# First pass of a four-layer graph kernel: statistics of two chunks of x earlier, a group's tail one chunk later, the weights' split in three pieces

## The chip, the core and the metric

One core of a Trainium2 chip. The metric is device time in microseconds (us) of one launch. TensorE is called PE below, VectorE DVE, ScalarE ACT, GpSimd POOL, and SyncE, which issues nearly all transfers, SP.

## What is computed

x has 4096 rows of 256, adj is a dense 4096 x 4096 matrix. Four graph layers follow each other, each with a layer norm before it and a residual behind it:

```python
h = relu(layernorm(x)); x = x + L0(h, adj, W)
    # L0: A2 = adj + I; d = diag(A2)**-0.5
    #     relu((d[:,None]*A2*d[None,:]) @ (A2 @ h @ W.T))
h = relu(layernorm(x)); x = x + L1(h, adj, weight, bias)   # softmax attention, weighted by adj
h = relu(layernorm(x)); x = x + L2(h, adj, W, b)           # relu(D^-1/2 adj D^-1/2 h @ W + b)
h = relu(layernorm(x)); x = x + L3(h, adj, W1, W2)         # two relu(concat(h, adj @ h) @ W)
```

All inputs and the output are f32.

## The kernel before

**Six passes over adj.** Each pass multiplies adj with a 4096 x 256 matrix: pass 0 is `A2 @ h` of the first layer, pass 1 its second product, pass 2 the attention, pass 3 the third layer, passes 4 and 5 the last one. An f32 matrix goes to PE as two f16 halves, hi (ACT, with a scale) and lo (DVE: the scaled value less hi), and a product is three matmuls: hi with hi, hi with lo, lo with hi.

**The first pass** (`first_pass`, L1206) is the only one that the change touches. adj is cut into 8 groups of 512 rows (`g`) and 8 chunks of 512 columns (`c`), 1 MB per chunk. The chunk (g, c) is loaded by SP into one of four ring slots (`load_at`, `load`), its hi half is made by ACT (L1487, in `split`), its lo half by DVE (L1939, in DVE's `split`); PE then runs 24 matmuls over 512 columns (`turned_block`, L1171 to 1173), or 48 over 256 and 128 columns if c equals g (`beside_corner`, L1186 to 1188), since the blocks on the diagonal, which get the identity added, are done apart (`corner_blocks`, L1203, after c = 7). From group 2 on DVE also makes two sums of quarters of each chunk (L1946, L1948) for later passes. Groups 0 and 1 (`PAIRED` = 2) run interleaved: chunk number n = 2c + g, so that n = 0 is (0, 0), n = 1 is (1, 0), n = 2 is (0, 1). From group 2 on n = 8g + c. PE takes the chunks in the order of n.

**The rows of x.** In group 0 chunk c of adj needs the normalised rows of chunk c of x (also 512 rows). They are made on the way, in a chain over three engines: DVE takes the statistics (`norm_stats`, the stage "stats" with p = PRE: bn_stats L2260 four times, bn_aggr L2265, L2267, L2268), POOL makes the power -1/2 and the shift (`rstd_of`, L1016, L1019), ACT writes relu of the normalised row in f16 and the normalised row in f32 (`first_rows`, L1631 and L1634, four rows of 128 each), and DVE makes the low half (L2081 row by row for chunks 0 to 2, L2093 for four at a time from chunk 3 on). PE waits for them row by row in chunks 0 to 2.

**Chunk 0** of adj comes in two halves: ACT makes two hi halves, DVE two lo halves (`split_first`, L2045), and PE begins its second half (k = 2) when the second is there.

**The tail of a group** is the product of its result with the layer's weights and its scaling. Its first half, "z", turns the sums in PSUM into hi and lo (ACT L1603, DVE L2052); PE then runs a small product (L1295 to 1297) after c = 2 of the next group; the second half, "t", turns its result into the moving matrix of pass 1 (ACT L1620, DVE L2069). `FIRST_PLACES` says behind which chunk of the next group ACT and DVE do each; the table stands once in ACT's program and once in DVE's. The groups 0 and 1 have their tails in group 2, by `TWO_PLACES`. The groups 4 to 7 are a loop, `first_group` twice per turn. The tail of group 7 lies in pass 1's first group, by the same table.

**The weights.** The first layer's are split early; the others (`wofs[1]` to `wofs[5]`, 3072 columns in one tensor) behind c = 5 of group 3, by one ACT instruction (L1460) and one DVE instruction (L2531). `w_ready` counts DVE's splits; POOL, PE and DVE wait for 2 before what follows.

**What sets the order.** Each engine has its own program, written out by hand, and works through it in order; semaphores tie them together. An engine that waits holds up everything behind it on that engine. So the order of DVE's program decides when each split and each row is ready.

Of the kernel before, what the change touches and what calls it, by code (L numbers as in the profile page):

```python
# [63 lines left out]
PAIRED = 2  # L64
# [6 lines left out]
PRE = -1  # L71
# [11 lines left out]
def build(nc, x, adj_t, w0, wg, bias_g, w2, bias_2, w3a, w3b, sent, sums, ready, x_mid, directs, out):  # L83
# [4 lines left out]
    with ctx:  # L88
# [125 lines left out]
        w_loaded = sem("w_loaded")  # L214
# [123 lines left out]

        PLAIN = [0, 1]

        def chunk_no(p, g, c):
# [661 lines left out]
        def _(pool):  # L1003
# [58 lines left out]
            add_identity(PAIRED + 1, 1)  # L1062
            pool.wait_ge(w_ready, 2)
            nc.gpsimd.memset(mov[1][:, :, F:LO], 1.0).then_inc(ones_ready, 1)
# [11 lines left out]
        def _(pe):  # L1076
# [350 lines left out]
            for p in range(6):  # L1427
                if p == 1:

                    pe.wait_ge(w_ready, 2)  # L1430
                    pe.wait_ge(ones_ready, 2)
# [22 lines left out]
        def _(act):  # L1454
# [344 lines left out]

            FIRST_PLACES = {0: "z", 3: "t"}  # L1800
            TWO_PLACES = {0: ("z", 0), 3: ("t", 0), 4: ("z", 1), 7: ("t", 1)}

            def first_group(g, side):

                for c in range(NC):
# [6 lines left out]
                    if c == 6:  # L1812
                        hi_of_corner(g, side)
                    if isinstance(g, int) and g == PAIRED + 1 and c == 5:
                        hi_of_weights(slice(wofs[1], wofs[5]), w_loaded, 16 * 4)

# [109 lines left out]
        def _(dve):  # L1926
# [498 lines left out]

            FIRST_PLACES = {0: "z", 3: "t"}
            TWO_PLACES = {0: ("z", 0), 3: ("t", 0), 4: ("z", 1), 7: ("t", 1)}

            def first_group(g, side):

                for c in range(NC):
# [6 lines left out]
                    if c == 6:  # L2438
                        lo_of_corner(g, side)
                    if isinstance(g, int) and g == PAIRED + 1 and c == 5:  # L2440
                        lo_of_weights(slice(wofs[1], wofs[5]), 2)

# [96 lines left out]
            lo_of_first_row(0, 0)  # L2539
            lo_of_first_row(0, 1)  # L2540
            split_first(1, split_ready, split_hi)
            lo_of_first_row(0, 2)
            lo_of_first_row(0, 3)
            stage("stats", PRE, 1)
            for q in range(NG):
                if q > 0:
                    split(0, 0, q)
                if q == 1:
                    lo_of_first_rows(1)
                    stage("stats", PRE, 2)  # L2550
                elif q == 2:
                    stage("stats", PRE, 3)
                    lo_of_first_rows(2)
                elif q > 2 and q + 2 < NG:
                    stage("stats", PRE, q + 2)
                elif q == NG - 1:
                    lo_of_corner(0, 0)
# [18 lines left out]
            dve.wait_ge(b_loaded, 32)  # L2576
            dve.wait_ge(w_ready, 2)
            for p in range(6):
# [56 lines left out]
```

## Time and profile before

| | us |
|---|---|
| median of 3 runs | 2312.75 |
| lowest and highest | 2312.53, 2313.29 |
| the profiled execution | 2313.05 |
| its span | 2311.3 |
| PE busy | 2289.8 (99%) |
| DVE busy | 1693.5 (73%) |
| ACT busy | 1127.9 (49%) |
| POOL busy | 145.9 (6%) |

The span runs from the first to the last instruction in the trace of one execution; its own time is that of the whole launch. In a row of the trace's order of time the first number is the start in us from the span's start, the second how long the row lasted; then follow engine, line, operation, what it writes and reads, the shape, and, in brackets, if the engine was idle before it, the idle time with what released it. A row of a stretch gives its start and end, its length, then the busy time and instructions of PE, PE's weight loads, DVE, ACT and POOL, the granted clock as a share of full speed, the busy share of the DMA engines and GB/s. A row of transfers gives what they move, their number, their size and the us from issue to landing.

### The profile page before, as it was taken

The page shows a single profiled execution, that of the slowest core. Times are in us where ns is not written, and L with a number is a line of the kernel's source. Part 1 is how long each engine was busy: PE and PEld are TensorE (multiplying, and loading weights), DVE is VectorE, ACT ScalarE, POOL GpSimd, SP SyncE. Part 2 cuts the span into 40 slices and gives each one's busy share as a digit, 9 for nine tenths or more (in the row PEclk, how much of TensorE's full clock was granted, in tenths as well). Part 3 has the DMA queues.
Part 4 walks back from the last instruction along what each step waited for, and adds up shares of the span by engine and source line. Part 5 has one row for each costly group of instructions (what it writes and reads, how often), then busy time and mean ns, then how long its engine had stood idle before and what let it go on. Part 6 is the DMA issues. An engine that isn't in the chain of part 4 may idle for free.

```text
span 2311.3 us, 61483 instructions
## 1 busy us (share of the span) xinstructions
PE 2289.8 (99%) x24200; PEld 1896.5 (82%) x24200; DVE 1693.5 (73%) x2709; ACT 1127.9 (49%) x1806; POOL 145.9 (6%) x139
## 2 busy tenths in 40 slices
PE   7999999999999999999999999999999999999999
PEld 4555557888888677778888899999988888899999
DVE  7678677676677788778888876776766667667666
ACT  7444434445544555555555555455454444433332
POOL 3300110111111000000000000000000000000000
PEclk9999999999999999999999999999999999999999
DMA  9989998889887898989999998998998998999998
GB/s 336 334 276 330 350 337 305 284 261 281 264 268 229 261 287 288 288 270 312 333 310 330 338 351 310 332 330 310 331 349 307 330 343 301 340 344 383 374 377 301
DMA packets 294894, 727.17 MB, mean 315 GB/s; under 512 B 77024, under 2 KB 114656, under 8 KB 262112
## 3 DMA queue, kind: packets, MB, share of 16 engines
q1 hardware_dynamic: 294608, 724.95, 90.6%
q8 instruction: 97, 1.59, 0.3%
q14 instruction: 45, 0.37, 0.0%
q10 hardware_dynamic: 144, 0.26, 0.0%
HBM read 574.64 MB, written 138.41 MB: 309 GB/s over the span
## 4 chain that ended last, share of the span: by engine, by line
PE 90%; DVE 5%; issue 2%; ACT 1%; DMA 1%; POOL 0%; SPq 0%; DVEq 0%; POOLq 0%; ACTq 0%
PE acc L1084 9%; PE acc L1086 8%; PE acc L1085 8%; PE acc L1110 8%; PE acc L1106 8%; PE acc L1109 8%; PE acc L1096 4%; PE acc L1099 4%; PE acc L1098 4%; PE acc L1171 4%; PE acc L1172 4%; PE acc L1173 4%; PE psS L1389 2%; PE psS L1391 2%; PE psS L1390 2%
## 5 line engine op out<-in xcount | busy, mean ns | idle before, releaser
L1084 PE MATMUL acc<-right,ahi 128*128 128x258 f16 x1024 | 279.7, 273 | 3.2 <-DVE alo L2502 2.8
L1086 PE MATMUL acc<-right,alo 128*128 128x258 f16 x1024 | 279.6, 273 | 0.0
L1085 PE MATMUL acc<-right,ahi 128*128 128x256 f16 x1024 | 279.1, 273 | 0.0
L1106 PE MATMUL acc<-left,ahi 128*128 128x128 f16 x1536 | 270.5, 219 | 0.4 <-DVE alo L2020 0.4
L1109 PE MATMUL acc<-left,ahi 128*128 128x128 f16 x1536 | 270.4, 219 | 0.0
L1110 PE MATMUL acc<-left,alo 128*128 128x128 f16 x1536 | 270.4, 219 | 0.0
L1867 ACT ACTIVATE ahi<-en 128x512 f16<-128x512 f32 x256 | 160.2, 626 | 76.2 <-DVE en L2487 74.0
L2502 DVE SCALAR_TENSOR_TENSOR alo<-en,ahi 128x512 f16<-128x512 f32 x256 | 176.0, 687 | 4.1 <-ACT ahi L1867 4.1
L1106 PE MATMUL acc<-left,adj 128*128 128x128 f16 x1024 | 178.2, 219 | 0.0
L1106 PE MATMUL acc<-left,en 128*128 128x128 f16 x1024 | 178.2, 219 | 0.0
L1109 PE MATMUL acc<-left,adj 128*128 128x128 f16 x1024 | 178.2, 219 | 0.0
L1109 PE MATMUL acc<-left,en 128*128 128x128 f16 x1024 | 178.2, 219 | 0.0
L1110 PE MATMUL acc<-left,adj 128*128 128x128 f16 x1024 | 178.2, 219 | 0.0
L1110 PE MATMUL acc<-left,en 128*128 128x128 f16 x1024 | 178.2, 219 | 0.0
L1106 PEld LDWEIGHTS acc<-left,ahi 128*128 128x128 f16 x1536 | 150.3, 98 | 0.7 <-DVE alo L2020 0.6
L1109 PEld LDWEIGHTS acc<-left,ahi 128*128 128x128 f16 x1536 | 150.3, 98 | 0.0
L1110 PEld LDWEIGHTS acc<-left,alo 128*128 128x128 f16 x1536 | 150.3, 98 | 0.0
L1548 ACT ACTIVATE ahi<-en 128x512 f16<-128x512 f32 x191 | 118.6, 621 | 54.6 <-DVE en L2015 54.5
L1084 PE MATMUL acc<-left,ahi 128*128 128x258 f16 x512 | 139.8, 273 | 0.0
L1086 PE MATMUL acc<-left,alo 128*128 128x258 f16 x512 | 139.8, 273 | 0.0
L1084 PE MATMUL acc<-left,en 128*128 128x258 f16 x512 | 139.8, 273 | 0.0
L1086 PE MATMUL acc<-left,en 128*128 128x258 f16 x512 | 139.8, 273 | 0.0
(313 smaller groups left out, 7036.9 us busy)
## 6 DMA issues: line engine op xcount, KB each, us to landing
adj<-in_adj_t SPq DMA_DIRECT2D x194, 512.0 KB, 5.8
adj<-ready SPq DMA_DIRECT2D x96, 1024.0 KB, 7.8
en<-ready SPq DMA_DIRECT2D x96, 1024.0 KB, 8.2
en<-in_adj_t SPq DMA_DIRECT2D x32, 1024.0 KB, 8.9
adj<-in_adj_t SPq DMA_DIRECT2D x31, 1024.0 KB, 7.5
en<-ready SPq DMA_DIRECT2D x56, 512.0 KB, 5.4
en<-sent SPq DMA_DIRECT2D x46, 512.0 KB, 7.2
sent<-en SPq DMA_DIRECT2D x90, 256.0 KB, 4.1
```

The source lines that it names most:

```text
L1084: nc.tensor.matmul(acc[:, b, 0:n], hi, m[:, jb, 0:n], start=first, stop=False)
L1085: nc.tensor.matmul(acc[:, b, 0:F], hi, m[:, jb, LO:LO + F], start=False, stop=False)
L1086: return nc.tensor.matmul(acc[:, b, 0:n], lo, m[:, jb, 0:n], start=False, stop=last)
L1096: nc.tensor.matmul(to, bhi[:, cols], hi[:, rows], start=first and i % 2 == 0 and k == 0, stop=False, skip_group_check=True)
L1098: nc.tensor.matmul(to, bhi[:, cols], lo[:, rows], start=False, stop=False, skip_group_check=True)
L1099: last = nc.tensor.matmul(to, blo[:, cols], hi[:, rows], start=False, stop=False, skip_group_check=True)
L1106: nc.tensor.matmul(to, hi[:, rows], bhi[:, cols], start=first and i % 2 == 0 and b == 0 and k == 0, stop=False, skip_group_check=True)
L1109: nc.tensor.matmul(to, hi[:, rows], blo[:, cols], start=False, stop=False, skip_group_check=True)
L1110: last = nc.tensor.matmul(to, lo[:, rows], bhi[:, cols], start=False, stop=False, skip_group_check=True)
L1548: nc.scalar.activation(ahi[:, c % 2, 2 * QUAD:3 * QUAD], s1_of(p, g, c), ACT.Copy, scale=ADJ_SCALE)\
L1867: nc.scalar.activation(ahi[:, (j // GB) % 2, j % GB * GR:(j % GB + 1) * GR], nums[:, n % NUMS, :], ACT.Copy, scale=P_SCALE).then_inc(num_h ...
L2502: nc.vector.scalar_tensor_tensor(alo[:, (j // GB) % 2, cols], nums[:, n % NUMS, :], P_SCALE, ahi[:, (j // GB) % 2, cols], ALU.mult, ALU.su ...
```

## The change

Four edits, all in the first pass:

1. DVE takes the statistics of x chunk 1 before the second half of adj chunk 0 and the low halves of rows 2 and 3, where it took them behind these.
2. DVE takes the statistics of x chunk 2 before the low halves of chunk 1, where it took them behind these.
3. `FIRST_PLACES` puts "t" behind c = 4 and not c = 3, on ACT and DVE, for groups 3 to 7 and for pass 1's first group.
4. The split of the later weights, one piece behind c = 5 of group 3, becomes three of 1024 columns each behind c = 1, 3 and 7 (`WEIGHTS_AT`), on ACT and DVE; the waits for `w_ready` 2 become waits for 4.

```diff
+        WEIGHTS_AT = {1: (wofs[1], wofs[3]), 3: (wofs[3], wofs[4]), 7: (wofs[4], wofs[5])}
...
-            pool.wait_ge(w_ready, 2)
+            pool.wait_ge(w_ready, 4)
...
-                    pe.wait_ge(w_ready, 2)
+                    pe.wait_ge(w_ready, 4)
...
-            FIRST_PLACES = {0: "z", 3: "t"}
+            FIRST_PLACES = {0: "z", 4: "t"}
...
-                    if isinstance(g, int) and g == PAIRED + 1 and c == 5:
-                        hi_of_weights(slice(wofs[1], wofs[5]), w_loaded, 16 * 4)
+                    if isinstance(g, int) and g == PAIRED + 1 and c in WEIGHTS_AT:
+                        hi_of_weights(slice(*WEIGHTS_AT[c]), w_loaded, 16 * 4)
...
-                    if isinstance(g, int) and g == PAIRED + 1 and c == 5:
-                        lo_of_weights(slice(wofs[1], wofs[5]), 2)
+                    if isinstance(g, int) and g == PAIRED + 1 and c in WEIGHTS_AT:
+                        lo_of_weights(slice(*WEIGHTS_AT[c]), 2 + list(WEIGHTS_AT).index(c))
...
             lo_of_first_row(0, 0)
             lo_of_first_row(0, 1)
+            stage("stats", PRE, 1)
             split_first(1, split_ready, split_hi)
             lo_of_first_row(0, 2)
             lo_of_first_row(0, 3)
-            stage("stats", PRE, 1)
             for q in range(NG):
                 if q > 0:
                     split(0, 0, q)
                 if q == 1:
+                    stage("stats", PRE, 2)
                     lo_of_first_rows(1)
-                    stage("stats", PRE, 2)
                 elif q == 2:
                     stage("stats", PRE, 3)
                     lo_of_first_rows(2)
```

The edit of `FIRST_PLACES` stands twice, once for ACT and once for DVE; so does the wait of DVE for `w_ready`. All lines behind the first edit move down by one.

**DVE at the start of the program.** `alo` of 128x1024 is a half of adj chunk 0, `alo` and `right` of 128x2048 are whole chunks (L1939), `right` of 128x256 are low halves of rows of x. Before, from the first half on:

```order
L2045 SCALAR_TENSOR_TENSOR alo<-adj,ahi 128x1024
L2081 SCALAR_TENSOR_TENSOR right<-o,right 128x256 x2
L2045 SCALAR_TENSOR_TENSOR alo<-adj,ahi 128x1024
L2081 SCALAR_TENSOR_TENSOR right<-o,right 128x256 x2
L2260 BN_STATS stats<-left 128x6 x4
L2265 BN_AGGR mv<-stats 128x2 x4
L2267 TENSOR_SCALAR nmean<-mv 128x4
L2268 TENSOR_SCALAR vare<-mv 128x4
L1939 SCALAR_TENSOR_TENSOR alo<-adj,ahi 128x2048
L1939 SCALAR_TENSOR_TENSOR right<-en,right 128x2048
L2081 SCALAR_TENSOR_TENSOR right<-en,right 128x256 x4
L2260 BN_STATS stats<-left 128x6 x4
```

Now:

```order
L2046 SCALAR_TENSOR_TENSOR alo<-adj,ahi 128x1024
L2082 SCALAR_TENSOR_TENSOR right<-o,right 128x256 x2
L2261 BN_STATS stats<-left 128x6 x4
L2266 BN_AGGR mv<-stats 128x2 x4
L2268 TENSOR_SCALAR nmean<-mv 128x4
L2269 TENSOR_SCALAR vare<-mv 128x4
L2046 SCALAR_TENSOR_TENSOR alo<-adj,ahi 128x1024
L2082 SCALAR_TENSOR_TENSOR right<-o,right 128x256 x2
L1940 SCALAR_TENSOR_TENSOR alo<-adj,ahi 128x2048
L1940 SCALAR_TENSOR_TENSOR right<-en,right 128x2048
L2261 BN_STATS stats<-left 128x6 x4
```

The four statistics instructions moved ahead of the second half of chunk 0 with its two rows; the next block of statistics moved ahead of the four low halves of chunk 1.

**DVE in group 3, behind c = 1.** `wsp` are the weights, `left<-psW` and `left<-psT` the tail's second half; each chunk is a split and two sums. Before, from c = 2 to the split of c = 4:

```order
L1939 SCALAR_TENSOR_TENSOR right<-en,right 128x2048
L1946 TENSOR_TENSOR right<-en 128x512
L1948 TENSOR_TENSOR right<-right,en 128x512
L1939 SCALAR_TENSOR_TENSOR right<-en,right 128x2048
L1946 TENSOR_TENSOR right<-en 128x512
L1948 TENSOR_TENSOR right<-right,en 128x512
L2069 SCALAR_TENSOR_TENSOR left<-psW,d_w,left 128x256 x2
L2069 SCALAR_TENSOR_TENSOR left<-psT,d_w,left 128x256 x2
L1939 SCALAR_TENSOR_TENSOR alo<-adj,ahi 128x2048
```

Now:

```order
L2532 SCALAR_TENSOR_TENSOR wsp<-left,wsp 128x1024
L1940 SCALAR_TENSOR_TENSOR right<-en,right 128x2048
L1947 TENSOR_TENSOR right<-en 128x512
L1949 TENSOR_TENSOR right<-right,en 128x512
L1940 SCALAR_TENSOR_TENSOR right<-en,right 128x2048
L1947 TENSOR_TENSOR right<-en 128x512
L1949 TENSOR_TENSOR right<-right,en 128x512
L2532 SCALAR_TENSOR_TENSOR wsp<-left,wsp 128x1024
L1940 SCALAR_TENSOR_TENSOR alo<-adj,ahi 128x2048
L1947 TENSOR_TENSOR right<-adj 128x512
L1949 TENSOR_TENSOR right<-right,adj 128x512
L2070 SCALAR_TENSOR_TENSOR left<-psW,d_w,left 128x256 x2
```

Two pieces of the weights stand ahead of the chunks c = 2 and c = 4, and the tail's second half moved behind c = 4. On ACT the same two moves are made.

## Rows read from the trace of the kernel before

**Rows 1.** Stretch from 371 us: PE, PEld, DVE, ACT, POOL busy (instructions), clock, DMA, GB/s

```profile
371.00:2311.30 1940.30, 1931.90 (x22072) 1704.24 (x22069) 1423.45 (x2392) 949.10 (x1621) 81.14 (x80) 1.00 0.91 312
```

**Rows 2.** The page: span, and granted TensorE clock in 40 slices

```profile
span 2311.3 us, 61483 instructions
...
PEclk9999999999999999999999999999999999999999
```

**Rows 3.** PE in order of time: first matmul of chunks 1 to 6

```profile
17.92 0.39 PE L1171 MATMUL acc<-ahi,right 128*128 128x512 f16 x1 [1.93 <-DVE alo L1939]
...
23.11 0.38 PE L1171 MATMUL acc<-right 128*128 128x512 f16 x1
...
29.02 0.28 PE L1186 MATMUL acc<-right 128*128 128x256 f16 x1 [0.57 <-DVE right L1939]
...
33.76 0.38 PE L1171 MATMUL acc<-ahi,right 128*128 128x512 f16 x1 [0.60 <-DVE right L2081]
...
39.49 0.39 PE L1171 MATMUL acc<-ahi,right 128*128 128x512 f16 x1 [0.39 <-DVE alo L1939]
...
46.41 0.39 PE L1171 MATMUL acc<-right 128*128 128x512 f16 x1 [1.57 <-DVE right L1939]
```

**Rows 4.** PE, first matmul of chunks 26, 27, 28, and of group 4's chunks three to five

```profile
158.25 0.38 PE L1171 MATMUL acc<-right 128*128 128x512 f16 x1
...
166.05 0.27 PE L1186 MATMUL acc<-right 128*128 128x256 f16 x1
...
171.27 0.39 PE L1171 MATMUL acc<-ahi,right 128*128 128x512 f16 x1 [1.10 <-DVE alo L1939]
...
211.50 0.38 PE L1171 MATMUL acc<-right 128*128 128x512 f16 x1
...
216.84 0.28 PE L1186 MATMUL acc<-ahi,right 128*128 128x256 f16 x1
...
220.81 0.38 PE L1171 MATMUL acc<-ahi,right 128*128 128x512 f16 x1
```

**Rows 5.** DVE in order of time, 11 to 22 us

```profile
11.50 1.22 DVE L2045 SCALAR_TENSOR_TENSOR alo<-adj,ahi 128x1024 f16<-128x1024 f32 x1
...
13.46 1.40 DVE L2260 BATCH_NORM_STATS2 stats<-left 128x6 f32<-128x256 f32 x4
...
15.57 2.29 DVE L1939 SCALAR_TENSOR_TENSOR alo<-adj,ahi 128x2048 f16<-128x2048 f32 x1
...
21.28 0.42 DVE L2081 SCALAR_TENSOR_TENSOR right<-en,right 128x256 f16<-128x256 f32 x1 [1.21 <-ACT en L1634]
```

**Rows 6.** ACT in order of time, 20 to 25 us

```profile
20.15 0.60 ACT L1631 ACTIVATE right<-left,shift,rstd 128x256 f16<-128x256 f32 x1 [3.46 <-POOL shift L1019]
...
24.10 1.89 ACT L1487 ACTIVATE right<-en 128x2048 f16<-128x2048 f32 x1
```

**Rows 7.** POOL in order of time, 15 to 34 us

```profile
15.75 2.98 POOL L1016 TENSOR_TENSOR rstd<-vare,neghalf 128x4 f32<-128x4 f32 x1 [7.56 <-DVE vare L2268]
...
33.36 1.11 POOL L1016 TENSOR_TENSOR rstd<-vare,neghalf 128x4 f32<-128x4 f32 x1 [2.14 <-DVE vare L2268]
```

**Rows 8.** DMA issues from 2.0 to 2.6 us, and landings of line 567's seven loads

```profile
left<-in_x SPq DMA_DIRECT2D x1, 512.0 KB, 6.7
...
DMA to landing us min/median/max: 6.7/10.2/13.9
```

**Rows 9.** PE: the warming matmuls, and where chunk 0's second half begins

```profile
6.95 4.42 PE L1420 MATMUL acc<-ident 128*128 128x128 f16 x40 [6.95 <-DVE vare L2268]
...
13.85 0.27 PE L1186 MATMUL acc<-ahi,right 128*128 128x256 f16 x1
```

**Rows 10.** DVE in order of time: splits of chunks 26 and 28, and the weights

```profile
154.51 2.28 DVE L1939 SCALAR_TENSOR_TENSOR right<-en,right 128x2048 f16<-128x2048 f32 x1
...
168.92 2.29 DVE L1939 SCALAR_TENSOR_TENSOR alo<-adj,ahi 128x2048 f16<-128x2048 f32 x1 [0.92 <-ACT ahi L1487]
...
175.99 3.35 DVE L2531 SCALAR_TENSOR_TENSOR wsp<-left,wsp 128x3072 f16<-128x3072 f32 x1
```

More of the change, by code:

```diff
@@ L2424, in first_tail @@
                     lo_of_t(g)
-            FIRST_PLACES = {0: "z", 3: "t"}
+            FIRST_PLACES = {0: "z", 4: "t"}
             TWO_PLACES = {0: ("z", 0), 3: ("t", 0), 4: ("z", 1), 7: ("t", 1)}
@@ L2576, in _ @@
             dve.wait_ge(b_loaded, 32)
-            dve.wait_ge(w_ready, 2)
+            dve.wait_ge(w_ready, 4)
             for p in range(6):
```

## The prediction, made before the changed kernel ran

> **What bounds the kernel now.** I read the page first, then the PE rows of the first pass in order of time, then what DVE, POOL and ACT did in front of each hole. PE is the clock of this program: in the 1940 us after the first pass it is busy for 1931.90 of 1940.30 us [rows 1], at a granted clock of full speed in every slice [rows 2]. A microsecond counts only if PE itself loses it, and the change touches only the first pass, so the question is how much PE loses there.
>
> To see that, one takes start to start, not the bracketed idle time, because a matmul's row overlaps the next by 0.16 us. An ordinary chunk of the first pass (24 matmuls over 512 columns) takes 23.11 - 17.92 = 5.19 us [rows 3]. The chunk on the diagonal (48 narrower ones) takes 220.81 - 216.84 = 3.97 us [rows 4]. I number chunks in PE's order: 0 to 15 are the paired groups 0 and 1, 24 to 31 are group 3. Against that:
> - chunk 2, 23.11 to 29.02: 5.91, so 0.72 lost before chunk 3
> - chunk 3 (diagonal), to 33.76: 4.74, so 0.77 lost before chunk 4
> - chunk 4, to 39.49: 5.73, so 0.54 lost
> - chunk 5, to 46.41: 6.92, so 1.73 lost
> - chunk 27 (diagonal), 166.05 to 171.27: 5.22, so 1.25 lost
> - group 4, its fourth chunk, 211.50 to 216.84: 5.34, so 0.15 lost, and the same in groups 5, 6 and 7.
>
> The releasers named in the brackets are DVE's splits (right or alo, L1939) and once a row of x (L2081) [rows 3, 4]. So in the early holes DVE is late. Why it is late stands in three views. DVE is out of work for 1.21 us at 21.28, waiting for ACT's normalised rows of x chunk 1 [rows 5]; ACT had waited 3.46 us for POOL's shift [rows 6]; and POOL's power took 2.98 us beside a DVE split, where a later one took 1.11 [rows 7]. It is one chain: statistics, power, rows, low halves, next split.
>
> **The change, part by part.**
>
> *Statistics of chunk 1 ahead of the second half of adjacency chunk 0.* The block of statistics costs DVE 15.57 - 13.46 = 2.11 us, the half split 1.22 [rows 5]. The block now starts at 11.50, so its x must have landed: that load was issued at 2.15 and took 6.7 us [rows 8], there at 8.9. The half split then runs 13.61 to 14.83 and two rows of 0.42 follow; DVE's work up to 15.57 is the same, so chunk 1's split still starts at 15.57 and PE still starts chunk 1 at 17.92. The price is that PE, which went on with chunk 0's second half at 13.85 [rows 9], now waits until about 15.2. That half took 2.1 us (to 17.92 - 1.93 = 15.99 [rows 3]), so it ends near 17.3, before 17.92: the hole of 1.93 us is cut in two and the term is **0**. Nothing else is queued behind it on PE.
>
> POOL gets the variance at 13.6 and not 15.6. Bounds: 1.11 us for the power if DVE leaves it alone, 2.98 if not [rows 7]. In both cases shift is there by about 17.9 at the latest, since DVE's next long split ends at 17.86 [rows 5]. ACT is free at 20.15 - 3.46 = 16.7 and needs 24.10 - 20.15 = 3.95 us for the eight activations of a chunk [rows 6]: done between 20.6 and 21.9, against 24.1.
>
> *Statistics of chunk 2 ahead of the low halves of chunk 1.* DVE is done with chunk 2's split at 15.57 + 2 x 2.29 = 20.15 and goes straight on: statistics to 22.26 (its x, issued at 3.8, landed by 17.7 even with the longest landing of all, 13.9 us [rows 8]), four low halves of 0.42 to 23.9, all inputs there. The rest, with the same durations, ACT's 1.89 for a split [rows 6], and PE's need from 17.92 on:
> - chunk 3: split done 26.2, PE needs it at 28.3: the 0.72 goes
> - chunk 4: split 28.5, statistics of chunk 3 30.6, first row 31.1, needed at 32.3: the 0.77 goes
> - chunk 5: rows to 32.3, split 34.6, needed at 37.5: the 0.54 goes
> - chunk 6: ACT reaches its rows of x chunk 3 at 33.4 (rows of chunk 2 to 29.6, two splits), or 35.5 if POOL is held up twice; rows done 37.4 to 39.5, DVE's low half about 1.2, split 2.29: done 40.9 to 43.0, needed at 42.7. The 1.73 goes, or 0.3 of it stays.
>
> Later paired chunks have what they need earlier too, since SP reissues a ring slot as soon as DVE has split it. Sum: 0.72 + 0.77 + 0.54 + 1.73 = **3.76 us**. Late next is chunk 6, with 1.8 us to spare or none.
>
> The SBUF page of the Trainium skill (SBUF — State Buffer, "Who interferes with whom") says that a DVE instruction with two SBUF inputs and a GpSimd one that reads SBUF exclude each other for a whole instruction, and that issue order decides who blocks. Here the long power rows fit the case in which DVE was first [rows 7]. By the rule the other order is possible too, and by it DVE would be set back by a whole power before chunk 1: the sum would be 4.5 and not 5.6, the second rival below.
>
> *A tail's second half one place later.* In group 3 chunk 28's split stood behind the tail's low halves and started only at 168.92 [rows 10]; PE wanted it at 166.05 + 3.97 = 170.0 [rows 4]. Now it goes ahead of the tail. Its adjacency chunk is requested right after chunk 24's split, some 20 us before, so only DVE's queue decides. Two chunks cost DVE 175.99 - 168.92 = 7.07 us there, 3.54 each [rows 10]: chunk 26 from 155.7 (with the piece of the weights below), chunk 27 to 162.8, the second piece to 164.0, chunk 28's split done at 166.3. Chunk 29 stands behind the tail now: sums to 167.6, four low halves of about 0.5 to 169.6, split done 171.9, needed at 170.0 + 5.19 = 175.2. **1.25 us** go, and in groups 4 to 7 4 x 0.15 = **0.6 us**. The tail's own result is not needed before the next tail, 211.50 - 166.05 = 45 us on [rows 4], or the next pass. In the second pass's first group the tail also moves; PE has no hole there, so 0. The cover is the 5.19 us that each chunk gives DVE.
>
> *The weights in three pieces.* 3.35 us in one instruction of 3072 columns [rows 10] become three of about 1.12 to 1.22 (the 1024-column form [rows 5]); the work is the same. Behind chunk 25 the first piece puts chunk 26's split at 154.51 + 1.22 [rows 10], done 158.02, and PE takes it at 158.25 [rows 4]: covered by 0.2 us, the thinnest place of the change. If POOL's identity additions stretch it, 0.1 to 0.3 us are lost. The second piece is in the times above, the third stands at the group's end, where DVE leads by 4 us. POOL's and PE's waits for four instead of two increments end near 181 against an end of the pass at 371: 0. Alone this part is worth 0.
>
> **Sum.** 3.76 + 1.25 + 0.6 = 5.6 us off, of which I take all. The profiled execution took 2313.05 us (span 2311.3), the median of the runs is 2312.75, 0.3 less; 2312.75 - 5.6 = **2307.1 us**. A measurement of this kernel tells apart some 0.2%, 4.6 us, so "faster" begins below 2308.1, and there is 1 us of room.
>
> **Rivals.**
> - *The gain is partly given back later* (0.13). DMA is 0.91 busy in the later stretch and PE idles 8.4 us there [rows 1]. If some of those idle spots are set by transfers that do not move with PE, they grow. For it: the high share. Against it: transfers start when a buffer comes free, so they move along, and 8.4 us in 1940 is little. Half of it given back: 2309.9.
> - *POOL or the thin places take their share* (0.13). DVE is held by a power that starts first (1.1), or chunks 6 and 26 come late (0.3 each). Against: beside the power at 15.75 the DVE split at 15.57 took its usual 2.29 [rows 5, 7]. About 1.2 us less: 2308.3.
> - *The clock falls* (0.05). PE began at the lower level, 40 matmuls over 128 columns in 4.42 us, 0.11 us each, that is 1.2 GHz [rows 9]; 5.19/24 = 0.216 us for 512 columns is 2.4 GHz [rows 3]. The new hole comes at 13.85, shortly after the rise. If the clock falls back there for as long as it took to rise, at most 13.85 - 6.95 = 6.9 us, PE loses half of that, 3.45, less the 0.7 that it has in hand before chunk 1: 2307.1 + 2.8 = 2309.9. Against: a hole of 1.93 us at 16 was followed by full speed, and now it is split into 1.35 and 0.6. The page TensorE: Matmul & The Clock Gate of the Trainium skill ("What's actually happening") has the level depend on how busy PE has lately been; by that rule too the shorter holes are the milder case.
> - *Slower than before* (0.03). The same fall, but lasting: from the point where more than 2 x (5.6 + 0.7) = 12.6 us run at half rate the change loses. At 20 us PE loses 10, less the 0.7: 2307.1 + 9.3 = 2316.4. The rows speak against it, since after chunk 1 PE would be without holes, and it rose once from a start that was no busier.
> - *It does not do what it says*: the statistics come sooner, but rows of x do not, because POOL is held until the same split ends. Then only the later terms stay, 1.85 us: 2310.9 (0.04). Even the fully blocked case above gains 2.2 us on ACT, so I give it little.
>
> **The numbers.** The forecast (0.62) has 2306.4 to 2308.1 as its own range. Reaching to the first three rivals gives 2305.9 to 2310.0. Faster takes the forecast and a third of the second rival, 0.66; slower 0.03; the rest 0.31.
>
> **What would show it.** Right: PE rows at 17.9, 23.1, 28.3, 32.3, 37.5, 42.7 without brackets but for the first, a hole of about 1.3 us near 14, ACT's rows of chunk 1 starting by 17.9, chunk 28 starting 3.97 us behind chunk 27. Wrong: chunk 1 later than 18.2, a hole before chunk 6 or 26, matmul rows of 0.42 us after 13, or PE idle after the first pass above 9 us.

## The result, and the profile after

| | before | after |
|---|---|---|
| median, 13 runs each | 2312.75 us | 2307.0 us |
| lowest and highest | 2312.19, 2313.29 | 2306.12, 2308.56 |
| the profiled execution | 2313.05 | 2306.9 |
| its span | 2311.3 | 2305.0 |

The ratio is 0.9976, with a 95% interval of 0.9969 to 0.9983: 5.75 us off, where 5.6 were forecast. The gain is clear of 1, but the interval reaches over 0.998, the line below which the prediction counts a kernel as faster, so the measurement does not settle that.

The stretch from the start of the second pass to the end, in the columns of [rows 1]:

```profile
365.00:2305.00 1940.00, 1931.96 (x22075) 1704.44 (x22072) 1422.44 (x2392) 948.63 (x1622) 81.15 (x80) 1.00 0.90 312
```

PE is busy for 1931.96 of 1940.00 us, before for 1931.90 of 1940.30. Its idle time went from 8.40 to 8.04 us, and the DMA share from 0.91 to 0.90. Nothing was given back later, so nearly all of the gain lies in the first pass. A hole is a stretch in which PE is idle; its bracketed time stands in the row of the matmul behind it. PE in the first pass, in order of time, the first matmul of each stage (the first row shows the warming matmuls, the second is the second half of chunk 0, then come chunks 1 to 6):

```profile
7.02 4.42 PE L1421 MATMUL acc<-ident 128*128 128x128 f16 x40 [7.02 <-DVE vare L2269]
...
15.43 0.28 PE L1187 MATMUL acc<-ahi,right 128*128 128x256 f16 x1 [1.43 <-DVE right L2082]
...
17.96 0.39 PE L1172 MATMUL acc<-ahi,right 128*128 128x512 f16 x1 [0.38 <-DVE alo L1940]
...
23.15 0.38 PE L1172 MATMUL acc<-right 128*128 128x512 f16 x1
...
28.33 0.27 PE L1187 MATMUL acc<-right 128*128 128x256 f16 x1
...
32.29 0.38 PE L1172 MATMUL acc<-ahi,right 128*128 128x512 f16 x1
...
37.47 0.38 PE L1172 MATMUL acc<-ahi,right 128*128 128x512 f16 x1
...
42.65 0.38 PE L1172 MATMUL acc<-right 128*128 128x512 f16 x1
```

Against [rows 3] the four holes before chunks 3 to 6 are gone. From chunk 1 on the starts are 5.18 or 5.19 us apart, 3.96 for the diagonal chunk 3. Chunk 6 starts at 42.65 and not at 46.41, 3.76 us sooner. The hole of 1.93 us before chunk 1 has become one of 1.43 inside chunk 0 and one of 0.38 before chunk 1, and chunk 1 starts where it did.

Group 3 and group 4 (chunks 26, 27 and 28, then group 4's fourth chunk and the diagonal one behind it), against [rows 4]:

```profile
154.34 0.38 PE L1172 MATMUL acc<-right 128*128 128x512 f16 x1
...
162.14 0.27 PE L1187 MATMUL acc<-right 128*128 128x256 f16 x1
...
166.10 0.38 PE L1172 MATMUL acc<-ahi,right 128*128 128x512 f16 x1
...
206.32 0.38 PE L1172 MATMUL acc<-right 128*128 128x512 f16 x1
...
211.50 0.27 PE L1187 MATMUL acc<-ahi,right 128*128 128x256 f16 x1
```

Chunk 28 stands 3.96 us behind chunk 27, where it stood 5.22 behind. The step of 5.34 in group 4 is 5.18 now, and the like losses of groups 5 to 7, in front of 261.19, 305.53 and 349.88 before, are gone too. Counting the lead from stage to stage, in starts of PE: 3.76 us at chunk 6, 3.91 at chunk 27, 5.17 at chunk 28, 5.34 at group 4's diagonal chunk, 5.76 at the first matmul of the second pass (370.73 before, 364.97 now).

DVE at the same place, the first piece of the weights, the splits of chunks 26 and 28 and the tail, against [rows 10]:

```profile
150.53 1.22 DVE L2532 SCALAR_TENSOR_TENSOR wsp<-left,wsp 128x1024 f16<-128x1024 f32 x1
151.67 2.28 DVE L1940 SCALAR_TENSOR_TENSOR right<-en,right 128x2048 f16<-128x2048 f32 x1
...
159.86 2.28 DVE L1940 SCALAR_TENSOR_TENSOR alo<-adj,ahi 128x2048 f16<-128x2048 f32 x1
...
163.39 0.87 DVE L2070 SCALAR_TENSOR_TENSOR left<-psW,d_w,left 128x256 f16<-128x256 f32 x2
```

Chunk 28's split is done at 162.14, 4 us ahead of PE; it was begun at 168.92 before. Chunk 26's is done at 153.95, 0.4 ahead.

DVE and ACT show why the early holes went. DVE, against [rows 5]:

```profile
11.71 1.40 DVE L2261 BATCH_NORM_STATS2 stats<-left 128x6 f32<-128x256 f32 x4
...
13.82 1.22 DVE L2046 SCALAR_TENSOR_TENSOR alo<-adj,ahi 128x1024 f16<-128x1024 f32 x1
...
15.62 2.28 DVE L1940 SCALAR_TENSOR_TENSOR alo<-adj,ahi 128x2048 f16<-128x2048 f32 x1
...
22.14 1.42 DVE L2082 SCALAR_TENSOR_TENSOR right<-en,right 128x256 f16<-128x256 f32 x4
23.87 2.29 DVE L1940 SCALAR_TENSOR_TENSOR right<-en,right 128x2048 f16<-128x2048 f32 x1 [0.31 <-ACT right L1488]
26.08 2.28 DVE L1940 SCALAR_TENSOR_TENSOR alo<-adj,ahi 128x2048 f16<-128x2048 f32 x1
...
39.39 2.28 DVE L1940 SCALAR_TENSOR_TENSOR right<-en,right 128x2048 f16<-128x2048 f32 x1
```

ACT and POOL, against [rows 6, 7]:

```profile
18.00 0.60 ACT L1632 ACTIVATE right<-left,shift,rstd 128x256 f16<-128x256 f32 x1 [1.10 <-POOL shift L1020]
```

```profile
13.99 1.92 POOL L1017 TENSOR_TENSOR rstd<-vare,neghalf 128x4 f32<-128x4 f32 x1 [5.74 <-DVE vare L2269]
15.98 1.98 POOL L1020 TENSOR_TENSOR shift<-nmean,rstd 128x4 f32<-128x4 f32 x1
22.31 1.11 POOL L1017 TENSOR_TENSOR rstd<-vare,neghalf 128x4 f32<-128x4 f32 x1 [4.34 <-DVE vare L2269]
```

The statistics of chunk 1 now start at 11.71 in place of 13.46, and ACT's rows of chunk 1 at 18.00 in place of 20.15. DVE's four low halves, which waited 1.21 us for ACT, now wait for nothing: they stand behind the statistics of chunk 2 and start at 22.14, and by then the rows are there. Chunk 6's split is done at 41.67, and PE takes it at 42.65: 1 us to spare.

### The profile page after: what moved, and what is told of

The parts are those of the page before. It is cut to its first block, busy times and chain, and to the rows that moved or that the text cites. A ratio compares the mean times of both kernels' runs of the same rounds, so it can differ in the third digit from the quotient of the medians.

```text
span 2305.0 us, 61487 instructions
## 1 busy us (share of the span) xinstructions
PE 2288.1 (99%) x24200; PEld 1897.1 (82%) x24200; DVE 1689.4 (73%) x2711; ACT 1129.0 (49%) x1808; POOL 139.7 (6%) x139
## 4 chain that ended last, share of the span: by engine, by line
PE 94%; DVE 4%; issue 1%; ACT 0%; DMA 0%; SPq 0%; DVEq 0%; ACTq 0%
PE acc L1085 9%; PE acc L1087 9%; PE acc L1086 9%; PE acc L1107 8%; PE acc L1110 8%; PE acc L1111 8%; PE acc L1097 4%; PE acc L1100 4%; PE acc L1099 4%; PE acc L1172 4%; PE acc L1174 4%; PE acc L1173 4%; PE psS L1390 2%; PE psS L1392 2%; PE psS L1391 2%; DVE alo L2503 1%
```

## The experiments

They were timed in four sets, each beside the kernel before, whose median was 2313.03, 2313.04, 2312.93 and 2312.71 us (33, 27, 24 and 14 runs). The sets ran on chips 5, 1, 0 and 5. The interval of each ratio reaches 0.0009 or 0.001 to either side, about 2 us. A difference between two of these kernels that is smaller than that is not settled by the medians; where it is called shown below, it is by the rows of the traces.

### The parts alone

**The two moves of the statistics alone.** The tables are as before:

```diff
-            FIRST_PLACES = {0: "z", 4: "t"}
+            FIRST_PLACES = {0: "z", 3: "t"}
...
-                    if isinstance(g, int) and g == PAIRED + 1 and c in WEIGHTS_AT:
+                    if isinstance(g, int) and g == PAIRED + 1 and c == 5:
```

> Only the two blocks of statistics are moved. Theory (DVE is late in the first 50 us and the rows of x are why): the four holes of PE before chunks 3 to 6 go, 3.8 us, and those near 171 us and of 0.15 us in groups 4 to 7 stay: 2309.0 us, chunk 1 starting at 17.9 as before, a hole of about 1.4 us near 14. Rival (the gain sits in the later stage, the tail's place and the weights): at most 1 us, 2311.8 or more. Rival (clock): some executions are 1 to 3 us above the others.

Measured: 2309.06 us (11 runs, ratio 0.9984, 0.9975 to 0.9993), 3.97 less than before, as expected. The early holes are gone, and the hole before chunk 28 stands as it was:

```profile
167.31 0.39 PE L1171 MATMUL acc<-ahi,right 128*128 128x512 f16 x1 [1.09 <-DVE alo L1939]
```

**The tail one chunk later alone.** `FIRST_PLACES` as in the change, all else as before.

> Only the tail's second half is moved from behind the fourth to behind the fifth chunk; the weights stay one piece. Theory: 1.25 us before chunk 28 and 4 times 0.15 us go, 1.85 in all: 2310.9 us, early holes as before; DVE has the piece of 3.35 us covered (chunk 30 split near 179, needed near 180). Rival (the pieces are needed for it): the whole piece behind chunk 29 makes PE wait before chunk 30, and nothing or less than 1 us is left.

Measured: 2311.13 us (11 runs, ratio 0.9992, 0.9983 to 1.0001), 1.9 less, as expected. The interval just includes 1, so it is the rows that show this term: the early holes stand (1.91 before chunk 1, 1.57 before chunk 6), and none stands before chunk 28 or in groups 4 to 7.

**The weights in three pieces alone.** `WEIGHTS_AT` as in the change, all else as before.

> Only the weights' split in three pieces, the tail's second half still behind the fourth chunk. Theory: the second piece now stands behind the tail and ahead of chunk 28's split, so that the hole there grows by the piece, about 1.0 to 1.1 us: 2313.8 us. Rival (the pieces free DVE and gain by themselves): 2312.75 or less.

Measured: 2313.8 us (11 runs, ratio 1.0007, 0.9998 to 1.0016), 0.8 more. With the tail still behind c = 3, the second piece stands between the tail and chunk 28's split, on ACT and on DVE. ACT of this kernel (its piece and the hi half of chunk 28), DVE (the tail's last low halves, its piece and the split), and PE at chunk 28, where the hole was 1.10 us before [rows 4]:

```profile
166.26 1.05 ACT L1461 ACTIVATE wsp<-left 128x1024 f16<-128x1024 f32 x1
167.20 1.91 ACT L1488 ACTIVATE ahi<-adj 128x2048 f16<-128x2048 f32 x1
```

```profile
166.40 0.88 DVE L2070 SCALAR_TENSOR_TENSOR left<-psT,d_w,left 128x256 f16<-128x256 f32 x2 [0.37 <-ACT left L1621]
167.34 1.23 DVE L2532 SCALAR_TENSOR_TENSOR wsp<-left,wsp 128x1024 f16<-128x1024 f32 x1
169.14 2.29 DVE L1940 SCALAR_TENSOR_TENSOR alo<-adj,ahi 128x2048 f16<-128x2048 f32 x1 [0.57 <-ACT ahi L1488]
```

```profile
171.49 0.39 PE L1172 MATMUL acc<-ahi,right 128*128 128x512 f16 x1 [2.04 <-DVE alo L1940]
```

DVE is through with its piece 0.57 us before the split starts, and what it waits for is ACT's hi half, which ACT makes behind its own piece. So here ACT is the late engine, and its piece, 0.94 us from start to start, is what the hole has grown by (2.04 - 1.10). The kernel before had the same order of lateness: its split of chunk 28 waited 0.92 us for ACT's hi half [rows 10], which ACT began at 166.98, right behind its tail. The change moves tail and pieces on both engines; no run moves them on one alone.

The runs fell in two heaps that nobody had expected: six from 2313.0 to 2313.8, and five from 2315.47 to 2315.86, these five at a mean granted clock of 0.998 or 0.999 (three of the other six are at 0.999 too, and so are 16 of the 33 runs of the kernel before, so 0.999 alone says little). The median of 2313.8 is the highest run of the lower heap, so that it met the expectation to the digit is partly luck. More on the heaps below.

**The change without the pieces.** Both moves and the later tail, the weights in one piece behind c = 5.

> The whole change without the split of the weights in three pieces: both moves of the statistics and the tail one chunk later, the weights in one piece of 3072 columns behind c = 5. Theory (the pieces are worth nothing once the tail is moved, and cost 0.8 without it, because the second piece then stands between the tail and chunk 28's split): 2306.9 to 2307.2, no hole in group 3. The sum of the two parts measured alone, 3.97 and 1.9, gives 2307.1. Rival (the one piece of 3.35 us, behind c = 5 and now one chunk nearer to the tail, makes a later chunk of group 3 late): 0.3 to 1 us slower than the whole change, 2307.3 to 2308, with a hole at chunk 29, 30 or 31.

Measured: 2306.92 us (10 runs, ratio 0.9976, 0.9966 to 0.9985), the time of the whole change, with no hole behind chunk 1 at all. The one piece of 3.35 us stands behind chunk 29 and its cover holds. So no gain or loss from the pieces shows once the tail is moved. The parts add up: 3.97 + 1.9 = 5.87 against the 5.79 of this kernel and the 5.75 of the whole change.

### What the first move is worth

**The change without its first move.** The statistics of chunk 1 go back behind the second half of chunk 0:

```diff
             lo_of_first_row(0, 1)
-            stage("stats", PRE, 1)
             split_first(1, split_ready, split_hi)
             lo_of_first_row(0, 2)
             lo_of_first_row(0, 3)
+            stage("stats", PRE, 1)
```

> The whole change except that the statistics of chunk 1 stay behind the second half of chunk 0. Theory: PE has no hole near 14 but one of 1.9 us before chunk 1, which starts at 17.9 as before; DVE makes the low halves of chunk 1 as ACT delivers them, to 24.6, splits of chunks 3 and 4 at 26.9 and 29.9, the first row of chunk 2 at 32.4 against 32.3 needed: at most 0.4 us are lost against the whole change, 2307.0 to 2307.4. Rival (the first move carries the early gain): the holes before chunks 3 to 6 come back, 2309 or more. On the clock: if the hole near 14 is what lets some executions of the changed kernel come out at 2308 and not 2306.6, here they all lie within 1 us.

Measured: 2308.35 us (11 runs, ratio 0.9979, 0.997 to 0.9988), 1.35 above the whole change. The expectation missed: the median lies between the theory's range and the rival's, and the runs span 1.5 us and not 1. The profiled execution showed something else than a late row. PE at the start of chunk 1, and the stretches around it (columns as in [rows 1], the eighth number is the granted clock):

```profile
17.84 0.61 PE L1172 MATMUL acc<-ahi,right 128*128 128x512 f16 x1 [2.66 <-DVE alo L1940]
18.24 0.63 PE L1173 MATMUL acc<-alo,right 128*128 128x512 f16 x1
18.67 0.63 PE L1174 MATMUL acc<-ahi,right 128*128 128x512 f16 x1
...
20.73 0.38 PE L1173 MATMUL acc<-alo,right 128*128 128x512 f16 x1
...
24.40 0.38 PE L1172 MATMUL acc<-right 128*128 128x512 f16 x1
```

```profile
16.00:19.00 3.00, 1.16 (x3) 0.43 (x4) 3.00 (x2) 0.62 (x1) 2.92 (x2) 0.70 1.04 421
19.00:22.00 3.00, 3.00 (x11) 1.19 (x10) 2.82 (x11) 1.92 (x4) 1.04 (x1) 0.73 1.01 415
22.00:25.00 3.00, 3.00 (x15) 1.37 (x14) 1.61 (x6) 3.00 (x6) 1.40 (x2) 1.00 0.97 377
```

Behind a hole of 2.66 us the first matmuls start 0.42 us apart and not 0.216, which is 1.2 GHz and not 2.4, and the granted clock of the two stretches is 0.70 and 0.73. Chunk 1 takes 24.40 - 17.84 = 6.56 us and not 5.19, 1.37 lost. Behind it there is no hole, and chunk 6 starts at 43.90, 1.25 later than in the whole change. Read from this one execution, the loss is the clock's. The next run tells whether it is.

**The same with PE kept busy in that hole.** 30 small matmuls ahead of PE's wait for chunk 1; `keep_warm(n)` issues n matmuls of 128 columns on the identity, whose result nobody reads:

```diff
                     else:
+                        if n == 1:
+                            keep_warm(30)
                         pe.wait_ge(split_ready, n + 1)
```

> The change without its first move, as in the run before, with 30 such matmuls between chunk 0 and chunk 1, where the profile of that run showed a hole of 2.7 us and then the clock at its lower level. Theory (its 1.3 us above the changed kernel are the clock's): it comes to within 0.4 us of the changed kernel, chunk 1 takes 5.2 us and not 6.6. Rival (the first move of the statistics is worth 1 us by itself): it stays near 2308.3.

Measured: 2308.24 us (11 runs, ratio 0.9979, 0.997 to 0.9988), 1.33 above the whole change in the same set, as the rival said. The mean granted clock is 1.0 in all 11 runs, where it was 0.999 in 5 of the 11 of the run before. So the clock is not the reason. Chunk 1 takes 23.37 - 18.18 = 5.19 us here, at full speed, and the time comes back as holes. PE at chunks 1, 4 and 6, and ACT's first row of chunk 1 with the split it delays on DVE:

```profile
18.18 0.39 PE L1172 MATMUL acc<-ahi,right 128*128 128x512 f16 x1 [0.98 <-DVE alo L1942]
...
33.37 0.38 PE L1172 MATMUL acc<-ahi,right 128*128 128x512 f16 x1 [0.60 <-DVE right L2084]
...
44.14 0.39 PE L1172 MATMUL acc<-right 128*128 128x512 f16 x1 [0.25 <-DVE right L1942]
```

```profile
20.41 0.60 ACT L1634 ACTIVATE right<-left,shift,rstd 128x256 f16<-128x256 f32 x1 [3.46 <-POOL shift L1020]
```

```profile
26.29 2.29 DVE L1942 SCALAR_TENSOR_TENSOR right<-en,right 128x2048 f16<-128x2048 f32 x1 [1.37 <-ACT right L1490]
```

Without the first move ACT waits for POOL's shift for 3.46 us, as before [rows 6], and everything behind it on ACT and DVE is over 2 us late: chunk 3's split starts at 26.29 and not at 23.87. It waits there for ACT's hi half of chunk 3, which ACT makes behind its eight rows of x, at 24.36. From chunk 1 to chunk 6 PE needs 44.14 - 18.18 = 25.96 us against 42.65 - 17.96 = 24.69, 1.27 more. Where the clock fell, PE was late by about as much, and DVE's lateness was hidden behind it. The two losses are of about one size, and one covers the other.

### The hole inside chunk 0, and a better version

**The whole change again**, in the set of the run before and of the next two.

> The changed kernel itself, beside the next three on the same chip: 2307.0 us, with a few executions about 1.3 us above the rest.

Measured: 2306.91 us (9 runs, 2306.04 to 2308.31, ratio 0.9974, 0.9964 to 0.9984).

**Two of the four statistics of chunk 1 in DVE's idle time.** DVE waited 0.29 and 0.48 us for the rows of chunk 0 around 11; two of the bn_stats go in there:

```diff
-            lo_of_first_row(0, 0)
-            lo_of_first_row(0, 1)
-            stage("stats", PRE, 1)
+            dve.wait_ge(x_loaded[1], 16)
+            for b in range(2):
+                nc.vector.bn_stats(stats[:, b, :], x_rows(PRE, 1)[:, b, :]).then_inc(stats_ready, 1)
+                lo_of_first_row(0, b)
+            norm_stats(PRE, 1, done=2)
```

> The whole change, and two of the four bn_stats of chunk 1 put into DVE's idle spots ahead of the low halves of rows 0 and 1. Theory (after the change only DVE's work before 15.6 us sets when PE starts chunk 1): the hole near 14 and chunk 1's start both come 0.6 to 0.7 us earlier, chunk 6 still has its input in time: 0.6 us less than the changed kernel. Rival (something else, ACT or a landing, is next in line within 0.2 us): less than 0.3 us.

Measured: 2306.63 us (9 runs, 2305.99 to 2307.86, ratio 0.9973, 0.9963 to 0.9983), 0.28 below the whole change, half of what was expected and less than the runs scatter. In the profiled executions PE starts chunk 1 at 17.60 here and at 17.52 in the whole change of the same set; but the first half of adj was split later here, on DVE at 9.06 against 8.51. Counted from there, chunk 1 comes 8.54 us on and not 9.01, 0.47 sooner. DVE was free for chunk 1's split at 15.16, but there ACT is next in line: its split of chunk 1 ran from 13.32 to 15.2, and DVE's started at 15.25. The rest of what is missing is less than these runs can tell.

**Small matmuls in the hole inside chunk 0.**

```diff
+                        if n == 0 and k == GB // 2:
+                            keep_warm(20)
```

> The whole change, with 20 matmuls of 128 columns on the identity, whose result nobody reads, in PE's new hole in chunk 0. Theory (DVE-bound hole): they fit, 20 times 0.055 us at the higher level is 1.1 us, and the fastest executions stay where they are. Theory of the clock: the slower executions of the changed kernel are ones in which the clock fell after a hole at the start; with the hole filled there are none above 2307.3, and the median drops by 0.2 to 0.5 us. Rival (the slower executions have another cause): the spread stays.

Measured: 2306.96 us (9 runs, 2306.29 to 2307.42, ratio 0.9975, 0.9965 to 0.9984). The median is that of the whole change, and not 0.2 to 0.5 below it. No run lies above 2307.42, where 5 of the whole change's 22 did (2308.03 to 2308.56), three of these at a mean clock of 0.999. That would fit a clock that falls in some executions, but 0 of 9 against 5 of 22 can be chance, and in the same set it is 0 against 1 of 9. Against it: three other kernels here have that hole and do not fill it (1.10 us with two bn_stats earlier, 0.54 with the weights in one piece, 1.14 with two pieces, below), and none of their 29 runs lies above 2308. What the late runs of the whole change have in common stays open.

**Both together.**

> The whole change, with two of the four bn_stats of x chunk 1 put into DVE's idle time ahead of the first half of chunk 0, and 20 small matmuls in the hole inside chunk 0. The first of these alone gave 2306.63 (fastest 2305.99), the second alone 2306.96 with no run above 2307.42. Theory (the gains are independent, the second takes away only late runs): median 2306.4 to 2306.7, no run above 2307.5. Rival (what the later runs have in common is not the hole in chunk 0): median as before, some of the runs above 2307.5.

Measured: 2306.65 us (9 runs, 2305.78 to 2307.54, ratio 0.9973, 0.9963 to 0.9983). The median is in the expected range, and one run lies just above 2307.5. It is 0.3 us below the changed kernel and level with the first of the two alone (2306.63). That is no difference that nine runs settle.

### The thinnest place

**The weights in two pieces, 2048 columns behind c = 1.**

```diff
-        WEIGHTS_AT = {1: (wofs[1], wofs[3]), 3: (wofs[3], wofs[4]), 7: (wofs[4], wofs[5])}
+        WEIGHTS_AT = {1: (wofs[1], wofs[4]), 7: (wofs[4], wofs[5])}
```

> The whole change, but the weights' split in two pieces: 2048 columns behind c = 1, 1024 behind c = 7. DVE's piece behind c = 1 takes about 2.4 us in place of 1.2, and the split of chunk 26 (the chunk behind the small product's place) was ready 0.4 us before PE took it at 154.34. Theory (DVE's lateness behind c = 1 is passed on to PE without loss elsewhere): chunk 26 starts 0.8 us later, with a hole of 0.8 before it, and no hole at chunk 28; 2307.8, 0.8 above the whole change. Rival (the small product gives way, or DVE catches up by its waits): within 0.3 of the whole change, 2306.9 to 2307.3, and no hole at chunk 26.

Measured: 2307.21 us (10 runs, ratio 0.9975, 0.9966 to 0.9985), 0.2 to 0.3 above the whole change's medians in two other sets. DVE's piece and the split of chunk 26 behind it, and PE at chunk 26:

```profile
149.70 2.29 DVE L2532 SCALAR_TENSOR_TENSOR wsp<-left,wsp 128x2048 f16<-128x2048 f32 x1
151.90 2.29 DVE L1940 SCALAR_TENSOR_TENSOR right<-en,right 128x2048 f16<-128x2048 f32 x1
```

```profile
154.24 0.39 PE L1172 MATMUL acc<-right 128*128 128x512 f16 x1 [0.38 <-DVE right L1940]
```

By the place the theory holds: the cover breaks and PE waits before chunk 26, 0.54 us from start to start. By the size the rival is nearer. In this execution PE was 0.65 us sooner than in the changed kernel's (chunk 25 at 148.51 against 149.16), as it was from chunk 1 on, and DVE 0.83 (150.53 against 149.70 at the piece). The 0.18 between them comes nearly all from POOL: in the changed kernel's execution DVE's first sum behind the split of chunk 25 took 0.94 us beside a POOL addition, here 0.68, while the split before it took 2.36 and 2.46. Of the 1.07 us by which the piece is longer, the margin of 0.39 and these 0.16 take their part, which leaves 0.52, against the 0.54 measured.

### The clock behind a late hole

**The three pieces alone, with small matmuls in the hole before chunk 28**, in a bank that the first pass does not use:

```diff
+                        if n == 3 * NC + 4:
+                            for _ in range(28):
+                                nc.tensor.matmul(psS[:, 1, 0:P], ident[:, :], ident[:, :], start=True, stop=True)
```

> The weights' pieces alone, with 28 small matmuls (128 columns, into a bank that the first pass does not use) ahead of PE's wait for chunk 28, in the hole of 2.04 us at 171.49 in which the same kernel without them was a us later in the median and, in 5 of its 11 runs, 2.2 us later with a mean granted clock of 0.998 or 0.999. Theory (the hole is long enough that the granted clock falls behind it in some executions): all runs between 2313.0 and 2314.0 with a clock of 1.0, median about 2313.3. Rival (the later runs have another cause, such as a transfer that lands late): a similar part of the runs, 3 or more of 9 to 11, again above 2315.

Measured: 2313.68 us (11 runs, ratio 1.0003, 0.9994 to 1.0012), all between 2312.9 and 2314.06; the median was expected at 2313.3 and all clocks at 1.0, but 7 of the 11 are at 0.999. The hole is filled:

```profile
169.49 1.73 PE L1216 MATMUL psS<-ident 128*128 128x128 f16 x28
171.69 0.39 PE L1172 MATMUL acc<-ahi,right 128*128 128x512 f16 x1 [0.48 <-DVE alo L1943]
```

PE does the same work and waits for the same split, only it is busy meanwhile, and the second heap is gone (0 of 11, before 5 of 11). That supports a clock that falls behind this hole in some executions, at a price of 2 us. It is not shown. No trace has it, since the profiled execution of the kernel without them was one of the first heap, and the two kernels ran in different sets, this one on chip 0 and the other on chip 5. That chip alone does not make a second heap: none of the 33 runs of the kernel before in the same set, whose hole is 1.10 us, lies above 2313.57.

## Why the prediction was right

**The bound.** PE's own holes in the first pass were the matter: PE's lead at the start of the second pass is 5.76 us and the medians differ by 5.75. That the two agree to 0.01 is luck. The same two profiled executions differ by 6.15 in their times, and from one execution of the changed kernel to another chunk 1 starts at 17.96 or 17.52, with the landing of adj's first half.

**First move, term 0.** Chunk 1 starts at 17.96, forecast 17.92; the hole near 14 is 1.43, forecast about 1.3; shift was forecast "by about 17.9 at the latest" and is there at 17.96, the fully blocked case. The term of 0 is right for chunk 1 and misleading for the move: undone alone it costs 1.3 us, by the run with PE kept busy. The prediction's second part had used the early rows of x without booking them to the move. The sum was right, the division was not. The expectation for the kernel without the first move had another slip: it let DVE split chunk 3 right behind the last low half at 24.6, to be done at 26.9, and left out that ACT's hi half of chunk 3 stands behind the rows. In its trace the split ends at 28.25. The second move was not taken out alone, so its own share is not measured.

**Second move, 3.76.** This term is that of both moves together. The lead at chunk 6 is 3.76. The forecast ends of DVE's splits against the measured ones: chunk 3 26.2 and 26.16, chunk 4 28.5 and 28.36, chunk 5 34.6 and 34.01, chunk 6 40.9 to 43.0 and 41.67. Both moves alone gave 3.97.

**The tail, 1.25 + 0.6.** Measured from start to start 1.26 at chunk 28 and 0.16 in group 4. The tail alone gave 1.9. The size is right, but the account named DVE's queue where ACT came last (the 0.92 in [rows 10]); it came out because the tail moves on both engines. Two small terms were not in the sum: before chunk 25 the old kernel lost 0.12 us (147.76 to 153.06 is 5.30), which is gone (POOL's part in it stands under the rivals), and group 7 has a new loss of 0.08 before its second chunk. They make a part of the 0.15 between 5.6 and 5.75; the rest is less than the runs can tell.

**The pieces, 0.** Right in the whole, by the run with one piece. "Alone this part is worth 0" was wrong: alone it costs 0.8 us by the medians, and the hole before chunk 28 grows by 0.94. The second piece was reckoned only with the tail behind it, and not in the order of the old tail. The first piece's margin at chunk 26, forecast 0.2, is 0.4 (153.95 against 154.34).

**The rivals.** No gain was given back later: PE idles 8.04 us, not above 9. No split of DVE was stretched beside POOL's power or shift, and no hole stands before chunk 6 or 26. The rule of the Trainium skill (SBUF — State Buffer, "Who interferes with whom") fits what POOL's rows show: the power of 1.92 us ends 0.87 us behind DVE's half split (15.91 against 15.04), and the shift of 1.98 ends 0.06 behind DVE's next split (17.96 against 17.90). In both DVE had started first. The other order, in which POOL holds up DVE, did not occur beside the power or the shift, but it did in group 3, beside POOL's identity additions. DVE and POOL of the kernel before, at chunk 25 (the split, the first sum, then POOL's four additions together and the last of them):

```profile
150.44 2.56 DVE L1939 SCALAR_TENSOR_TENSOR alo<-adj,ahi 128x2048 f16<-128x2048 f32 x1 [1.04 <-ACT ahi L1487]
152.93 0.94 DVE L1946 TENSOR_TENSOR right<-adj 128x512 f32<-128x512 f32 x1
```

```profile
149.57 3.75 POOL L1054 TENSOR_TENSOR ev<-ev,ident 128x128 f32<-128x128 f32 x4 [49.72 <-DMA ev<-in_adj_t]
150.82 2.50 POOL L1054 TENSOR_TENSOR ev<-ev,ident 128x128 f32<-128x128 f32 x1
```

The additions start 0.42 us apart, so the split started while the third ran; it took 2.56 us and not 2.28; it ends at 153.00, and PE started chunk 25 at 153.06, 0.12 late. Without the 0.28 the split would have been in time, and the other traces bear this out: in the execution of the pieces alone it took 2.29 and PE lost nothing there, in that of the tail alone 2.53 and PE lost 0.09. So the old loss of 0.12 goes back to POOL's additions. In the changed kernel's execution the same split took 2.36 and its cover held. This is the prediction's "POOL's identity additions stretch it", one chunk earlier than forecast. The clock did not fall in the profiled execution, and no trace of the changed kernel shows a fall. That it falls in some others would fit the run-to-run scatter, which is 2.4 us after and was 1.1 before, but it is not shown.

**The margin.** Faster was to begin below 2308.1, and the median is at 2307.0. Three of the 13 runs lay above that line, and the upper end of the interval, 0.9983, is 2308.8 us. So the size was forecast well, but "faster", which was given 0.66, is not what the measurement settled.

## What to carry to other kernels

When the bounding engine idles between stages, take its losses from start to start, name for each the engine that is late, and follow that one back to the instruction that stands in the wrong place of its program. A move of an instruction is worth what the whole chain behind it gains, so book each move by taking it out of the finished order, not by the first stage that it touches. Where work of no urgency has to go somewhere, put it where the queue has a lead, and never between a late stage and the split that the bound waits for.

## What was not expected of the hardware

- The clock's answer to nearly the same hole differs between executions. Behind the hole of 2.66 us at 17.84, in the kernel without the first move, a chunk took 6.56 us in place of 5.19. Behind one of 2.56 us in front of the same chunk, in the run with the pieces alone and small matmuls at chunk 28, the rows are at full speed (the second starts 0.23 us behind the first):

```profile
17.53 0.39 PE L1172 MATMUL acc<-ahi,right 128*128 128x512 f16 x1 [2.56 <-DVE alo L1943]
17.76 0.38 PE L1173 MATMUL acc<-alo,right 128*128 128x512 f16 x1
```

  With the hole of 2.04 us at 171.49 five of eleven runs were 2 us later, and with the same hole filled none of eleven.
- The length of an early hole goes with the time at which the clock rose. The order of DVE's work up to there is the same in the kernel with the statistics alone and in the whole change, but the hole inside chunk 0 is 2.26 us in the one and 1.43 in the other. In the one, PE ran the first half of chunk 0 in 2.0 us from 10.98 on; in the other it began at 11.23 with rows over 256 columns 0.21 us apart (0.11 at full speed) and took 2.6.
- Keeping PE busy through the hole in the kernel without the first move gained nothing (2308.35 without, 2308.24 with the small matmuls), though the profiled execution without them had the clock fall and the one with them had not, since DVE was late by as much.
- POOL's power, an instruction on 4 elements per partition, took 1.92 us beside DVE's split of 1024 columns and 2.98 beside one of 2048, while DVE's splits stayed at 1.22 and 2.28. With DVE idle it took 1.01 or 1.02, and beside four of DVE's low halves, 0.42 us each, 1.11. Each time it ended 0.86 or 0.87 us behind the DVE instruction that was running when it started: 15.91 against 15.04 and 23.42 against 22.56 in the changed kernel, 18.73 against 17.86 before [rows 5, 7]. So a short DVE instruction costs it next to nothing and a long one all that is left of it. In group 3 POOL's additions did stretch a split, to 2.56.
